# Heads in another order on TensorE: the score products of an attention layer, and the units of its probabilities

## What is computed

```
qkv = jnp.einsum('bld,ed->ble', x, W_qkv)          # B=32, L=65, D=512
q, k, v = ...                                      # H=16 heads of dh=32
q = _apply_rope(q); k = _apply_rope(k)
att = jnp.einsum('bhqd,bhkd->bhqk', q, k) * scale
att = jnp.where(causal, att, -jnp.inf)
p = jax.nn.softmax(att, axis=-1)
y = jnp.einsum('bhqk,bhkd->bhqd', p, v)
return jnp.einsum('ble,de->bld', y, W_o)
```

## Time and profile before

| | |
|---|---|
| median of 3 runs | 2843.27 us |
| the profiled execution | 2851.02 us |
| its span, first to last instruction | 2849.2 us |
| attention stage, from its first scores | 2277.6 us to the end, 572 us |
| mean granted TensorE clock, whole span | 0.918 |
| TensorE busy in that stage | 502.4 us of 572.2 |
| score products (L1820), busy | 59.2 us, 1024 records |
| value products (L1856), busy | 50.3 us, 1024 records |
| TensorE idle before the transposes L1847, waiting for ScalarE's copies | 28.4 us, 29 times |

### The profile page before, as it was taken

One profiled execution on the slowest core, in us unless ns is written; L12 is line 12 of the kernel. 1 busy time (PEld: TensorE's weight loads), 2 busy tenths in 40 slices (PEclk: granted clock), 3 DMA queues, 4 the chain that ended last, 5 costly groups with the idle time before them and its releaser, 6 DMA issues. The chain is left out here.

```text
span 2849.2 us, 48591 instructions
## 1 busy us (share of the span) xinstructions
PE 2412.6 (85%) x17080; PEld 2050.4 (72%) x17081; DVE 1937.1 (68%) x2921; ACT 1405.3 (49%) x3474; POOL 1215.1 (43%) x774
## 2 busy tenths in 40 slices
PE   4999987788888888888887764999999579999986
PEld 4999987788878887888876752444444467877775
DVE  7666436999999999999999781222222376776652
ACT  0342447888888888888888320111111123434332
POOL 3300003666666666666666572000000355454331
PEclk9998998999999999999999856999999778999986
DMA  5910000000000000000000263656553221111000
GB/s 189 411 70 1 1 1 31 31 31 32 31 32 31 32 31 32 32 32 32 31 32 31 81 192 96 192 177 238 179 182 115 64 61 44 33 45 32 9 9 16
DMA packets 65440, 209.57 MB, mean 74 GB/s; under 512 B 12224, under 2 KB 17600, under 8 KB 62400
## 3 DMA queue, kind: packets, MB, share of 16 engines
q1 hardware_dynamic: 24832, 95.96, 9.8%
q0 software_dynamic: 28576, 89.16, 9.7%
q10 hardware_dynamic: 11808, 21.50, 2.0%
HBM read 129.96 MB, written 76.62 MB: 73 GB/s over the span
## 5 line engine op out<-in xcount | busy, mean ns | idle before, releaser
L848 POOL TENSOR_TENSOR m_hs<-m_hs,m_BC 128x1040 f32<-128x1040 f32 x256 | 619.1, 2418 | 382.7 <-DVE m_hs L961 382.7
L767 ACT ACTIVATE m_dA<-m_dt,m_A 128x128 f32<-128x128 f32 x2048 | 614.4, 393 | 185.9 <-DVE m_hs L961 111.4
L642 PE MATMUL m_py<-m_hs,ident 128*128 128x130 f32 x4096 | 531.2, 285 | 147.0 <-POOL m_hs L848 146.8
L642 PEld LDWEIGHTS m_py<-m_hs,ident 128*128 128x128 f32 x4096 | 497.7, 197 | 166.9 <-POOL m_hs L848 164.9
L961 DVE TENSOR_TENSOR_SCAN m_hs<-m_dA,m_own 128x1040 f32<-128x1040 f32 x256 | 593.1, 2317 | 35.5 <-ACT m_dA L767 22.5
L946 DVE TENSOR_TENSOR m_own<-m_BC,m_own 128x1040 f32<-128x1040 f32 x256 | 318.7, 1245 | 18.8 <-issue 4.9
L594 PE MATMUL m_pw<-m_xg,m_w_in 128*128 128x130 f32 x2048 | 269.7, 292 | 51.0 <-DVE m_xc L909 35.0
L594 PEld LDWEIGHTS m_pw<-m_xg,m_w_in 128*128 128x128 f32 x2048 | 260.6, 207 | 54.6 <-DVE m_xc L909 38.0
L1446 PE MATMUL e_pG<-ew_gu,e_xT 128*128 x656 | 235.8, 503 | 10.9 <-issue 7.3
L1426 POOL DMA_DIRECT2D e_x<-regions x80 | 42.9, 536 | 403.8 <-PE e_pX L1437 403.8
L1517 DVE TENSOR_TENSOR e_h<-e_g,e_pG 128x192 f32<-128x192 f32 x82 | 29.1, 354 | 230.1 <-ACT e_g L1488 230.1
(11 more groups left out here) (290 smaller groups left out, 4375.4 us busy)
## 6 DMA issues: line engine op xcount, KB each, us to landing
m_BC<-xs SPq DMA_DIRECT2D x16, 2080.0 KB, 9.8
slots<-a_zero POOLq DMA_DIRECT2D x48, 512.0 KB, 44.5
ew_gu<-in_gate_up_w SPq DMA_DIRECT2D x32, 768.0 KB, 5.1
e_x<-regions POOLq DMA_DIRECT2D x82, 256.0 KB, 3.0
slots<-e_y ACTq DMA_DIRECT2D x82, 256.0 KB, 2.6
regions<-a_zero POOLq DMA_DIRECT2D x16, 512.0 KB, 15.7
ew_d<-in_down_w SPq DMA_DIRECT2D x32, 256.0 KB, 5.6
out_h<-t_ho SPq DMA_DIRECT2D x8, 520.0 KB, 3.3
```

What stands on the lines that cost most here:

```text
L642: mm = pe.matmul(py[k % 2][:, 0:MT], ident[:, :], hs[u % NB][:, n, :], start=False, stop=(half == 1 and n == HN - 1))
L767: act.activation(images(dA[u % NB][:, n, :])[:, :, 1:TOK], images(dt[b][:, k, :])[:, :, 1:TOK], ACT.Exp, scale=A[:, at:at + 1]).then_inc(d ...
L848: pool.tensor_tensor(hs[u % NB][:, :, :], hs[u % NB][:, :, :], BC[b][:, ST + half * HN:ST + (half + 1) * HN, :], ALU.mult).then_inc(prod_r ...
```

## The change

In the score products, the twelve of row groups 0, 1 and 2 are no longer issued group after group (four of r = 0, four of r = 1, four of r = 2), but around the groups: r = 0, 1, 2, 0, 1, 2 and so on. The last of r = 1 still raises `rows_done`, and is followed by one more product, the last of r = 2. The four of row group 3 alternate no longer by pairs but between banks 0 and 1.

The units are no longer cut from the order in `S`, but from the order of the head's number h = 4i + r. Before, the column groups r of the heads were 0 0 0 0 3 3 | 1 1 1 1 3 | 3 2 2 2 2, now they are 0 1 2 3 0 1 | 2 3 0 1 2 | 3 0 1 2 3. The units keep their sizes 6, 5 and 5. The place of a head in `S`, in `pS` and in `pY` stays.

```
@@ combine_attention_and_linear
-    UNITS = (range(0, 6), range(6, 11), range(11, 16))
+    HEADS = [ORDER.index((i, r)) for i in range(FT) for r in range(HQ)]
+    UNITS = (HEADS[0:6], HEADS[6:11], HEADS[11:16])
...
-                for bank in range(2):
-                    for at in range(FT):
-                        mm = score(bank, at)
-                mm.then_inc(rows_done, 1)
                 for at in range(FT):
+                    score(0, at)
+                    mm = score(1, at)
+                    if at == FT - 1:
+                        mm.then_inc(rows_done, 1)
                     score(2, at)
                 pe.wait_ge(rows_done, g * GB + b + 1)
-                for bank in range(2):
-                    for at in range(FT, HB):
+                for at in range(FT, HB):
+                    for bank in range(2):
                         mm = score(bank, at)
...
                         mm = pe.matmul(pY[r * DH:(r + 1) * DH, i * TOK:(i + 1) * TOK], v[b][:, h * DH:(h + 1) * DH],
-                                       PT[u][:, at - unit[0], :], start=True, stop=True)
+                                       PT[u][:, unit.index(at), :], start=True, stop=True)
```

## The result

The changed kernel takes 2836.91 us (median of 20 runs, 2831.88 to 2842.66) beside 2845.28 us for the kernel before on the same chip (20 runs, 2838.01 to 2849.64). The ratio is 0.9974, 95% interval 0.9967 to 0.9981: 7.4 us faster, between 5.4 and 9.4. The forecast was 15.9 us. The sign is right, and 2836.91 us lies inside the range, but less than half of the gain arrived.

What follows compares the result with a forecast made beforehand. TensorE's projections carry most of the attention stage's chain of waits, with value and score bursts between; GpSimd or VectorE hold it elsewhere. Savings by image group sum to 15.9 us, from 2843.3 to 2827.4 us; range 2818.8 to 2840.

Steps and rivals of the forecast that it cites:

- Inside a burst: Attention score and value products on TensorE: one group's records chain at 57 ns (110 at half clock), different groups overlap.
- the look-ahead of some four records: Within TensorE's bursts: the old order's second group begins only after about five records of the first.
- three row groups do not run at once: Rival in the score products: their terms, 5.1 us, fall out, giving 2832.4 us; chance 12%.
- column groups gain nothing: Rival in the value products: overlap stays, only score terms remain, giving 2838.2 us; chance 8%.
- What lies on the path: Attention stage: burst savings on the chain of waits, counted by group of images, sum to 15.9 us.
- 24.2 us off TensorE: All value and score bursts in the stage: the fall in TensorE's own time, taken as the upper bound.
- group: Group of images in the attention stage; each of eight got its own saving, from 0 to 3.5 us.
- the range's lower end: 2818.8 us, the time if the whole 24.2 us of TensorE savings lies on the path.
- the slower rival: Linear layer behind the second image's value burst runs at half clock, 35 us in seven groups: 2862 us; chance 7%.
- Its sign of failure: Attention stage: the prediction is wrong if the mean granted clock falls.
- Waits take over: Rival: waits such as those for ScalarE's copies (28.4 us) grow; 2 to 8 us gain stay, about 2838; chance 13%.

Runs made afterwards that it cites:

- the two half changes: Each half of the change alone against the kernel before: only the new score-product order, ratio 0.9981; only the new units, 0.9964.
- the extra products: Two 200-column matmuls into unused columns in TensorE's wait before each group's first w_qk projection; ratio to before 0.9943 in the changed kernel, 0.9998 in the old one.
- before_fill: Kernel before plus two unused 200-column matmuls in TensorE's wait before the first w_qk projection: 2845.73 us, ratio 0.9998 to the kernel before.
- after_fill: Changed kernel plus two unused 200-column matmuls in TensorE's wait before the first w_qk projection: 2829.98 us, ratio 0.9943 to the kernel before.
- scores_only: Kernel before with only the new order of the score products, units as before: 2837.07 us, ratio 0.9981 to the kernel before.
- after_touch: Changed kernel plus one unused one-column matmul in TensorE's wait before the first w_qk projection: 2837.36 us, ratio 0.9962 to the kernel before.
- fill(2, 200): Two unused 200-column matmuls in TensorE's wait before the first w_qk projection; ratio to before 0.9943 and 0.9930 in the changed kernel, 0.9998 and 0.9993 in the old.
- fill(1, 128): One unused 128-column matmul in TensorE's wait before the first w_qk projection, added to the changed kernel: ratio to the kernel before 0.9944, then 0.9956.

## Why the prediction was right and wrong

**Inside a burst: right.** Value bursts of 0.94 us at full clock and 1.17 at half (forecast 0.95 and 1.17), score bursts of 1.36 (1.36). The half-clock score burst saves 0.47 us (0.43). Three row groups run at once, which no row had shown, and the look-ahead of some four records, which I had inferred and no run tests by itself, was enough of a model. Of the rivals, "three row groups do not run at once" and "column groups gain nothing" fall with these rows and with the two half changes. The rule of the Trainium skill that was weighed there ("TensorE: Matmul & The Clock Gate", Part 3: a weight load goes ahead only for another row group) would have had no gain from the units; they gave 10.2 us.

**What lies on the path: right in the sum, in part by luck.** The forecast was 24.2 us off TensorE and 15.9 us off the time. With the extra products in both kernels it is 22.9 us from first to last record and 17.5 us by the stage; by the medians 15.7 and 19.9 us. Group by group, forecast, plain change, and with the products in both (`before_fill` to `after_fill`):

| group | 1 | 2 | 3 | 4 | 5 | 6 | 7 | 8 | sum |
|---|---|---|---|---|---|---|---|---|---|
| forecast | 3.5 | 1.0 | 2.1 | 0 | 2.3 | 1.5 | 2.3 | 3.2 | 15.9 |
| plain | 5.8 | 1.3 | 1.5 | -2.0 | 1.1 | -0.3 | 0.2 | 2.6 | 10.2 (rounded) |
| with products | 5.9 | 1.5 | 0.5 | 1.8 | 2.3 | 1.7 | 1.4 | 2.3 | 17.4 |

Group 1 gave 2.4 us more than its bursts: it has 6.8 us less at half clock (34.1 to 27.3). Groups 4 to 7 are where the plain change lost: there the sum was 6.1 us and -1.0 arrived. With the products groups 5 and 6 come out as forecast. Elsewhere errors of both signs cancel: groups 1 and 4 give 2.4 and 1.8 us more, groups 3, 7 and 8 give 1.6, 0.9 and 0.9 less, and the time at half clock moves by up to 10.3 us in a group (the second, 17.1 to 6.8). A slip besides: the range's lower end, 2818.8 us, should be 2843.3 − 24.2 = 2819.1.

**The step that failed** is the one against the slower rival: "the two bursts are short beside the projections, which are unchanged". By it the sum put the projections' time at no change; they took 11.0 us more. It asked how long the bursts are; it should have asked what stands next to them. The score burst stands ahead of a wait, and what it gives up is added to idle time there. That is not the whole mechanism, since `scores_only` has the same waits and no more half-clock starts than before; but work put into this wait took the loss away. The prediction also looked at one place only, the linear layer behind the second value burst. It did slow down (73.1 to 77.5 us busy), but the larger part was at the first `w_qk` block, which no rival named: three more half-clock starts of 1.69 us, 5.1 us of the 5.3 that `w_qk` grew by. And the rival was built all or nothing, a whole layer at half clock and 35 us; what happened is its small form, 11.0 us of projection time, which took some 7.4 us of the stage (17.5 to 10.1, four executions) and left a gain. Its sign of failure was named and came true: the mean granted clock of the stage fell, 0.86 to 0.85.

**Waits take over: a small part at most.** The waits for ScalarE's copies stayed at 28.4 us, as forecast. The linear layer's wait for VectorE's sum grew from 0.5 to 4.2 us. VectorE's normalization is longer where more of GpSimd's subtraction falls beside it. In the fifth group it was 2.36 us long with 1.25 us of the subtraction, and in the changed kernel it is 3.38 us with 1.94:

```profile
2576.18 3.38 DVE L2111 TENSOR_TENSOR t_xl<-t_xl,t_rstd 128x1040 f32<-128x1040 f32 x1 [0.84 <-ACT t_rstd L1983]
```

This goes both ways: in the fourth group it fell from 2.40 to 1.24 us, and `before_fill`, without the change, has 3.40 in the fifth. And idle time ahead of `w_qk` and `w_f` grows as much with the extra products (7.9 to 13.1 us) as without (10.5 to 16.4), and there the gain arrives. So these waits belong to the part of the shorter bursts that was never on the path, for which the forecast had 8.3 us, and are not the loss.

What stays open: why the clock falls in one group and not in the next. In the changed kernel it fell in groups 2 and 4 to 7, with 1.11 to 1.61 us idle ahead, and not in group 3, with 1.14. Why it took both short bursts is open with it. So is how much of the loss a given execution shows. The plain change measured 0.9974, 0.9968 and 0.9953 on three chips, with six, five and four half-clock starts in the profiled executions; that the starts follow the scatter is likely by this order, but three points do not show it. Nor was it tried whether the old score order in the one burst ahead of the wait, with the new one elsewhere, would do as well as the extra products.

## What to carry to other kernels

When work on TensorE gets shorter, look at what stands right behind each shortened piece: if that is a wait for another engine, the saving becomes idle time, and the projections behind the wait can start at half clock. Sum the untouched groups of the two profiles as well as the changed ones; here they hid 11.0 of 27.6 us. A few throwaway products in such a wait cost nothing that can be told and brought back 7 to 9 us, but measure how much is needed: a third of that work left one half-clock start in one measurement and four in the next.

## What was not expected of the hardware

- With some 0.7 us of work in a wait of some 1.1 us, 16 records took 3.77 us behind it in all of groups 2 to 7; without it they took 5.46 in five of the six. It is no rule of the wait's length: one of the six kept the full clock all the same, and `scores_only` with the same waits kept it in four. Before the change, with 0.82 us idle and a longer burst ahead, four of seven such places kept it. The Trainium skill ("TensorE: Matmul & The Clock Gate", "HAM oscillation — how this bites in real kernels") tells of this loss for kernels that wait long for transfers and start at half clock each time. This trace agrees with the effect and shows it at waits of another engine, and much shorter ones.
- A product with one column did nothing for the clock (`after_touch`), though it is an instruction like the others.
- Value products that share all their rows run up to 15 records deep when neighbours differ in column group, and 19 weight loads fall into 0.44 us at half clock where there were 5.
- Two executions of one program can differ in which groups fall to half clock, while the two programs with `fill(2, 200)` repeated their stage within 0.3 us on chips on which their medians are 12 and 16 us apart. With `fill(1, 128)` the stage took 550.7 us on one chip and 557.9 on another.
